# Splitting the operands of two 1x1 convolutions in a four-layer image kernel

## What is computed

```python
x = x + L0(gn(x))   # pooled mean -> gate g = sparsemax(8 experts); w_eff = g @ experts; 1x1 conv with w_eff
x = x + L1(gn(x))   # 3x3 depthwise conv, bias, bn, relu, prune (channel kept if its max >= 4.0);
                    # 1x1 conv pw_w, bias, bn, relu, prune (0.001)
x = x + L2(gn(x))   # q, k, v; squared and normalised q and k; kv = k2n^T v; attn = v + q2n kv; attn @ Wln + b
x = x + box3x3(gn(x))  # mean of the 3x3 neighbourhood
```

## Time and profile before

| | us |
|---|---|
| median of 3 runs | 1646.85 (1644.88 to 1647.62) |
| the profiled execution | 1646.53 |
| its span, first to last instruction | 1644.9 |
| PE busy | 1517.3 (92%) |
| DVE busy | 1296.9 (79%) |
| ACT busy | 1186.2 (72%) |
| POOL busy | 304.0 (18%) |

### The profile page before, as it was taken

The page is one execution under the profiler, slowest core; times in us unless marked ns, Lnnn a source line. Parts: engine busy times, 40 slices in busy tenths (PEclk is TensorE's granted clock), DMA queues, the critical chain, the costliest instruction groups (busy, mean ns, idle before and its releaser), DMA issues.

```text
span 1644.9 us, 27605 instructions
## 1 busy us (share of the span) xinstructions
PE 1517.3 (92%) x9282; PEld 1219.7 (74%) x9282; DVE 1296.9 (79%) x2339; ACT 1186.2 (72%) x2440; POOL 304.0 (18%) x238
## 2 busy tenths in 40 slices
PE   4469999999999999999999999999999999999850
PEld 2247787888887877878887877888877878878750
DVE  5758888888988888888888888889888888885430
ACT  3357777887777778877787778877787778776530
POOL 1100022222221121222221221222211221211001
PEclk8679999999999999999999999999999999999975
DMA  4001044434334444433334444333434444333435
GB/s 144 22 20 40 21 99 99 98 62 94 82 80 95 78 98 98 82 74 86 89 79 90 86 98 98 73 84 78 89 87 78 98 98 79 67 72 67 80 72 96
DMA packets 47172, 132.70 MB, mean 81 GB/s; under 512 B 3857, under 2 KB 4881, under 8 KB 47122
## 3 DMA queue, kind: packets, MB, share of 16 engines
q0 software_dynamic: 26112, 77.08, 28.8%
q1 hardware_dynamic: 20914, 54.98, 8.8%
q10 hardware_dynamic: 96, 0.00, 0.0%
HBM read 29.29 MB, written 102.76 MB: 80 GB/s over the span
## 4 chain that ended last, share of the span: by engine, by line
PE 90%; DVE 4%; DMA 2%; ACT 2%; issue 1%; POOLq 0%; ACTq 0%; DVEq 0%
PE conv_ps L457 35%; PE tile_ps L610 12%; PE tile_ps L539 10%; PE conv_ps L598 9%; PE small_ps L585 4%; PE tile_ps L484 4%; PE tile_ps L471 3%; PE tile_ps L567 3%; PE tile_ps L506 3%; DMA out<-row_sums 2%; PE tile_ps L503 2%; PE tile_ps L536 2%; PE tile_ps L555 2%; DVE h L803 1%; PE small_ps L448 1%
## 5 line engine op out<-in xcount | busy, mean ns | idle before, releaser
L803 DVE SCALAR_TENSOR_TENSOR h<-xpad,dw_sb,h 128x784 f32<-128x784 f32 x512 | 492.5, 1029 | 0.0
L1270 POOL DMA_DIRECT2D out<-row_sums x96 | 115.6, 1204 | 491.9 <-DMA out<-row_sums 411.2
L610 PE MATMUL tile_ps<-k,xT 112*128 112x256 f32 x896 | 201.4, 383 | 0.0
L1280 POOL TENSOR_SCALAR pw_masked<-pw_sb,hmask 128x256 f32<-128x256 f32 x64 | 118.4, 1857 | 385.4 <-DVE hmask L811 377.0
L610 PEld LDWEIGHTS tile_ps<-k,xT 112*128 112x128 f32 x896 | 171.9, 193 | 22.2
L539 PE MATMUL tile_ps<-wqk,xn_parts 128*112 128x256 f32 x1344 | 187.4, 294 | 0.0
L992 ACT ACTIVATE junk<-x 128x784 bf16<-128x784 f32 x192 | 162.8, 851 | 26.7 <-DVE x L830 17.5
L457 PE MATMUL conv_ps<-h,pw_masked 128*128 128x392 f32 x512 | 176.3, 498 | 5.5 <-issue 5.5
L598 PE MATMUL conv_ps<-x,mixed 128*128 128x392 f32 (+1 forms) x512 | 176.5, 498 | 2.2 <-ACT mixed L1029 1.1
L539 PEld LDWEIGHTS tile_ps<-wqk,xn_parts 128*112 128x112 f32 x1344 | 169.5, 175 | 0.1
L457 PE MATMUL conv_ps<-xn_parts,w_out 128*128 128x392 f32 x768 | 151.0, 345 | 0.0
(11 more groups left out here) (141 smaller groups left out, 2631.8 us busy)
## 6 DMA issues: line engine op xcount, KB each, us to landing
out<-row_sums POOLq DMA_DIRECT2D x96, 784.0 KB, 7.1
x<-x SPq DMA_DIRECT2D x32, 784.0 KB, 5.5
out<-x SPq DMA_DIRECT2D x32, 784.0 KB, 3.5
expert_sb<-expert_rows SPq DMA_DIRECT2D x8, 256.0 KB, 5.1
x<-w_qk SPq DMA_DIRECT2D x1, 512.0 KB
x<-w_vT SPq DMA_DIRECT2D x1, 256.0 KB
x<-w_ln SPq DMA_DIRECT2D x1, 256.0 KB
pw_sb<-pw_wT SPq DMA_DIRECT2D x1, 256.0 KB
```

What stands on the lines that cost most here:

```text
L610: mm = nc.tensor.matmul(tile_ps[:, KX_BANK, i * C:(i + 1) * C], xT[:, m, half(i)], k2[:, m, :], start=(m == 0), stop=(m == M - 1))
L803: ins = nc.vector.scalar_tensor_tensor(acc, view, scalar, acc, ALU.mult, ALU.add)
L1270: pool.dma_start(out_dram[F.times(1)], rows, accum_op=ALU.add).then_inc(rows_added[n].of(F), 16)
L1280: nc.gpsimd.tensor_scalar(pw_masked[:, j, :], pw_sb[:, j, :], hmask[:, j:j + 1], 0.0, ALU.mult, ALU.add).then_inc(pw_masked_ready.sem, 1)
```

## The change

Both plain float32 products become products on split operands.

- `pointwise` now multiplies `pw_parts` (the unmasked weights, split once in the set-up) by `h_parts`. The mask goes onto h: ScalarE's `h_high` writes h times hmask as high part, VectorE's `h_low` the low part. `mask_weights` on GpSimd goes. `h_parts` and `q_parts` are one buffer, `hq_parts`.
- `mixed_conv` multiplies `mixed_parts` (high by `scaled_mix` on ScalarE, low by `mixed_low` on VectorE) by `x0_parts`. The high part of x is written by the pass on ScalarE that sums x (`x0_high`, which stood among the key squares as half of `x0_sum` and now stands ahead of `sum_squares(1, A)`); the low part by `x0_low` on GpSimd, a `tensor_tensor` of 784 elements for each half, behind `add_rows`. The column of means that rides along with the product is split too (`mean_columns`, `mean_lows`). `x0_parts` has one buffer, so `x0_high` of an image waits for the first convolution of the image before, and `mixed_conv` waits for `mixed_low`, `mean_lows` and `x0_low`.
- x3 and the scratch tile `over` lose their second buffers. ScalarE's `sum_over_h` of the first half moves behind `normalise_x3`.
- The last two images (TAIL = 2) take `box_in_tail`: VectorE does the whole box filter in ten additions of 784 elements, and SyncE stores each half of the image once. These two images have no accumulating DMAs.

```diff
-x0 = sb("x0", [P, 2, J, XW])
-mixed = sb("mixed", [P, J * C])
+x0 = sb("x0", [P, 2, J, HW])
+x0_parts = sb("x0_parts", [P, 2, J, XW], F32R)
+mixed_parts = sb("mixed_parts", [P, 2, J * C], F32R)
...
-pw_masked = sb("pw_masked", [P, J, C])
...
-q_parts = sb("q_parts", [P, 2, J, HW], F32R)
-x3 = sb("x3", [P, 2, J, HW])
+hq_parts = sb("hq_parts", [P, 2, J, HW], F32R)
+h_parts, q_parts = hq_parts, hq_parts
+x3 = sb("x3", [P, J, HW])
...
+        if E.active and not E.in_tail:
             sp.wait_ge(x3_ready.sem, x3_ready.at(E))
...
+            sp.dma_start(out_dram[E.times(1)], x3[:]).then_inc(stored.of(E), 16)
+        if F.in_tail:
+            for j in range(J):
+                sp.wait_ge(tail_step.sem, tail_step.at(F - (IMAGES - TAIL), 5 * (j + 1)))
+                sp.dma_start(out_dram[F.offset][:, j, :], x3_of(F)[:, j, :]).then_inc(tail_stored, 16)
 
...
     def pointwise(C_, halves):
-        pe.wait_ge(h_ready.sem, h_ready.at(C_))
-        pe.wait_ge(pw_masked_ready.sem, pw_masked_ready.at(C_))
+        pe.wait_ge(h_lo.sem, h_lo.at(C_))
         for j in halves:
             wait_free((C_ - 1, q2_ready, j + 1), (C_ + 1, x1_ready, j + 1))
-            conv_tile(j, [(pw_masked[:, i, :], h[:, C_.odd, i, :]) for i in range(J)]).then_inc(pw_mm.sem, 1)
+            conv_tile(j, by_parts(pw_parts, h_parts)).then_inc(pw_mm.sem, 1)
...
-        pe.wait_ge(mean_column.sem, mean_column.at(A))
-        pe.wait_ge(mixed_ready.sem, mixed_ready.at(A))
+        pe.wait_ge(mean_low.sem, mean_low.at(A))
+        pe.wait_ge(x0_lo.sem, x0_lo.at(A))
+        pe.wait_ge(mixed_lo.sem, mixed_lo.at(A))
         for j in range(J):
             wait_free((A - 2, y_ready, j + 1), (A - 1, x1_ready, j + 1))
-            for i in range(J):
-                for a in range(2):
-                    more = a
-                    mm = nc.tensor.matmul(conv_ps[:, 2 * j + a, 0:HALF + more],
-                                          mixed[:, i * C + j * P:i * C + (j + 1) * P],
-                                          x0[:, A.odd, i, a * HALF:(a + 1) * HALF + more],
-                                          start=(i == 0), stop=(i == J - 1), skip_group_check=True)
+            for n, (u, v) in enumerate(((0, 0), (0, 1), (1, 0))):
+                for i in range(J):
+                    for a in range(2):
+                        width = HALF + 2 * a
+                        mm = nc.tensor.matmul(conv_ps[:, 2 * j + a, 0:width],
+                                              mixed_parts[:, u, i * C + j * P:i * C + (j + 1) * P],
+                                              x0_parts[:, v, i, a * HALF:a * HALF + width],
+                                              start=(n == 0 and i == 0), stop=(u == 1 and i == J - 1),
+                                              skip_group_check=True)
             mm.then_inc(conv0_mm.sem, 1)
...
+        parts_of(pw_parts, pw_raw)
         parts_of(wqk, wqk_raw)
...
         nc.vector.tensor_scalar(hmask[:], h_over[:], 0.0, None, ALU.is_gt).then_inc(hmask_step.sem, 1)
+
+    def h_low(C_):
+
+        for j in range(J):
+            dve.wait_ge(h_hi.sem, h_hi.at(C_, j + 1))
+            nc.vector.scalar_tensor_tensor(h_parts[:, 1, j, :], h[:, C_.odd, j, :], hmask[:, j:j + 1],
+                                           h_parts[:, 0, j, :].bitcast(F32), ALU.mult,
+                                           ALU.subtract).then_inc(h_lo.sem, 1)
...
+    def mean_lows(A):
+
+        dve.wait_ge(mean_column.sem, mean_column.at(A))
+        nc.vector.tensor_tensor(x0_parts[:, 1, :, HW:XW], gn_avg[:, 0, 0:2].unsqueeze(2).to_broadcast([P, J, 2]),
+                                x0_parts[:, 0, :, HW:XW].bitcast(F32), ALU.subtract).then_inc(mean_low.sem, 1)
+
+    def mixed_low(A):
+
+        dve.wait_ge(mixed_hi.sem, mixed_hi.at(A))
+        for i in range(J):
+            cols = slice(i * C, (i + 1) * C)
+            nc.vector.scalar_tensor_tensor(mixed_parts[:, 1, cols], small_ps[:, cols], gn_r[:, 0, i:i + 1],
+                                           mixed_parts[:, 0, cols].bitcast(F32), ALU.mult,
+                                           ALU.subtract).then_inc(mixed_lo.sem, 1)
...
     def make_x3(E):
-        if (E - 2).active:
-            dve.wait_ge(stored.of(E - 2), stored.at(E - 2))
-            dve.wait_ge(x3pad_ready.sem, x3pad_ready.at(E - 2))
-        for j in range(J):
+        if (E - 1).active and not (E - 1).in_tail:
+            dve.wait_ge(stored.of(E - 1), stored.at(E - 1))
+        for j in range(J):
+            if (E - 1).active:
+                dve.wait_ge(x3pad_ready.sem, x3pad_ready.at(E - 1, j + 1))
             dve.wait_ge(attn_mm.sem, attn_mm.at(E, j + 1))
-            nc.vector.scalar_tensor_tensor(split(x3[:, E.odd, j, :]), conv_banks(j), b_out[:, j:j + 1],
+            nc.vector.scalar_tensor_tensor(split(x3_of(E)[:, j, :]), conv_banks(j), b_out[:, j:j + 1],
                                            split(x2[:, E.odd, j, :]), ALU.add, ALU.add,
                                            accum_out=gn_in[:, 3, j:j + 1]).then_inc(x3_ready.sem, 1)
...
+    def box_in_tail(F):
+
+        s, turn = tail_step, F - (IMAGES - TAIL)
...
+        for j in range(J):
+            pad, rows, done = x3pad[:, j], row_sums[:, j], 5 * j
+            inner, out = pad[:, 1:1 + H, 1:1 + W], x3_of(F)[:, j, :]
+            dve.wait_ge(x3pad_ready.sem, x3pad_ready.at(F, j + 1))
+            nc.vector.tensor_tensor(rows[:, 1:1 + H, :], pad[:, 1:1 + H, 0:W], inner, ALU.add).then_inc(s.sem, 1)
+            dve.wait_ge(s.sem, s.at(turn, done + 1))
+            nc.vector.tensor_tensor(rows[:, 1:1 + H, :], rows[:, 1:1 + H, :], pad[:, 1:1 + H, 2:2 + W],
+                                    ALU.add).then_inc(s.sem, 1)
+            dve.wait_ge(s.sem, s.at(turn, done + 2))
+            nc.vector.tensor_tensor(inner, rows[:, 0:H, :], rows[:, 1:1 + H, :], ALU.add).then_inc(s.sem, 1)
+            dve.wait_ge(s.sem, s.at(turn, done + 3))
+            nc.vector.tensor_tensor(inner, inner, rows[:, 2:2 + H, :], ALU.add).then_inc(s.sem, 1)
+            dve.wait_ge(s.sem, s.at(turn, done + 4))
+            nc.vector.tensor_tensor(image_rows(out), image_rows(out), inner, ALU.add).then_inc(s.sem, 1)
...
             sparsemax(A)
+            mean_lows(A)
         if t.first:
             setup_weights()
...
         if C_.active:
             h_mask(C_)
-        if F.active:
+        if F.in_tail:
+            box_in_tail(F)
+        elif F.active:
             box_row_sums(F)
+        if C_.active:
+            h_low(C_)
+        if A.active:
+            mixed_low(A)
         if D.active:
             reciprocal_sums(D)
...
     def mean_columns(A):
 
         act.wait_ge(gn_read.sem, gn_read.at(A))
-        nc.scalar.copy(x0[:, A.odd, :, HW], gn_avg[:, 0, 0:2]).then_inc(mean_column.sem, 1)
+        if (A - 1).active:
+            act.wait_ge(conv0_mm.sem, conv0_mm.at(A - 1))
+        nc.scalar.copy(x0_parts[:, 0, :, HW:XW], gn_avg[:, 0, 0:2].unsqueeze(2).to_broadcast([P, J, 2])
+                       ).then_inc(mean_column.sem, 1)
...
+    def x0_high(Z):
+
+        act.wait_ge(x_loaded.of(Z), x_loaded.at(Z))
+        if (Z - 1).active:
+            act.wait_ge(conv0_mm.sem, conv0_mm.at(Z - 1))
+        for j in range(J):
+            nc.scalar.activation(x0_parts[:, 0, j, 0:HW], x0[:, Z.odd, j, :], ACT.Identity,
+                                 accum_out=gn_in[:, 0, j:j + 1]).then_inc(x0_hi.sem, 1)
+
+    def q_high(C_, D):
+        if C_.active:
+            act.wait_ge(pw_mm.sem, pw_mm.at(C_))
+        elif (D - 1).active:
             act.wait_ge(attn_mm.sem, attn_mm.at(D - 1))
         act.wait_ge(qa_ready.sem, qa_ready.at(D))
...
+    def h_high(C_):
+
+        act.wait_ge(hmask_step.sem, hmask_step.at(C_))
+        if (C_ - 2).active:
+            act.wait_ge(attn_mm.sem, attn_mm.at(C_ - 2))
+        for j in range(J):
+            nc.scalar.activation(h_parts[:, 0, j, :], h[:, C_.odd, j, :], ACT.Identity,
+                                 scale=hmask[:, j:j + 1]).then_inc(h_hi.sem, 1)
...
@@ -1182,23 +1288,23 @@
             relu_h(C_, 0)
         if D.active:
             x2_high(D)
-        if C_.active:
-            sum_over_h(C_, 0)
         if F.active:
             normalise_x3(F)
         if C_.active:
+            sum_over_h(C_, 0)
             relu_h(C_, 1)
         if A.active:
             scaled_mix(A)
         if C_.active:
             sum_over_h(C_, 1)
+            h_high(C_)
...
         for m in range(M):
             if D.active:
                 square_k(D, m)
-            if Z.active and 0 < m <= 2 * J:
-                x0_sum(Z, m - 1)
+            if Z.active and 0 < m <= J:
+                x0_squares(Z, m - 1)
...
         if t.first:
             act.wait_ge(setup_dve, SETUP_DVE)
+        if Z.active:
+            x0_high(Z)
         if A.active:
             junk_free((C_, gn_sums[2]), (Z, gn_sums[0]))
             sum_squares(1, A, x1[:, A.odd], x1_ready)
         if D.active:
```

(25 more changed lines are left out.)

90 lines of the change are left out of this document (46 added, 44 removed).

## The result

| | before | after |
|---|---|---|
| time, median of 4 runs each | 1647.23 us | 1672.13 us |
| ratio (95% interval) | | 1.0155 (1.0137 to 1.0172) |
| span of the profiled execution | 1644.9 us | 1671.3 us |

The runs answer the forecast of 1670 us closely. More than the total, the parts of it count. I cut both spans at the same operation, the copy of the group means that opens `variances` (line 713 before, 744 after), numbered by step. The profiled execution of the changed kernel took 1674.25 us, 2.1 over its median, so the parts add up to 26.5 us and not to the 24.9 of the medians.

What follows compares the result with a forecast made beforehand. Two bounds of equal length: TensorE's own work and a 46.40 us cycle through PE, ACT and DVE. 1646.5 + 32 (full steps) + 19 (start) - 27.7 (end) = 1670 us; range 1650 to 1699.

Steps and rivals of the forecast that it cites:

- The ring: Cycle from attention_out to the next: PE 16.58, ACT 9.42, DVE 20.40, together 46.40 us, within 0.05 of PE's own work.
- PE's 1.96 us: Time PE saves a step, 0.97 in pointwise and 0.99 in mixed_conv; only 0.1 us shortens the cycle, at relu_y.
- GpSimd's subtraction: x0_low blocks the six taps behind q_scales: first operation passes beside make_x1 and scale_q, taps lose 1.3 us a step.
- VectorE's 2.95 us hidden: h_low, mixed_low and mean_lows add 2.95 us between attention_weights_low and q_scales, covered by DVE's waits of 2.02 and 2.56.
- d: Duration of one x0_low operation on GpSimd: taken as 1.5 us, between 0.98 and 1.97; the skill's rate scaled gives 1.72.
- my formula: Loss of the six taps to the x0_low pair, 2d - 1.73: 1.3 us, between 0.25 and 2.2.
- The full steps: Steps t = 4 to 30, each about 1.2 us longer than 46.45: 27 x 1.2 = +32 us.
- The start: Steps 0 to 3: +9.3 as PE waits for mixed_low, +6.8, then +3; together +19 us, 14 to 23.
- The end: Last images with box_in_tail: ten additions of 1.0 us, half-image stores of 3.0; span ends 27.7 us earlier.
- One sign: PE idle about 3 us a step, most of it ahead of attention_out, with DVE's attn_parts as releaser.
- Rival 3: Both x0_low operations land among the taps (scale_q blocked or third DMA late): 3.0 us a step, 1720 us; chance 16%.

Runs made afterwards that it cites:

- experiment 1: Changed kernel, but GpSimd subtracts x's low part for the first image only (numbers wrong): 1631.24 us, ratio 0.991 to the kernel before.
- experiment 3: Two of the six taps behind q_scales moved ahead of it: changed kernel 1613.94 us (0.9797), kernel before 1644.12 us (0.9985).
- experiment 4: Changed kernel with the first of the first convolution's three products done twice, 8 more matmuls a step: 1674.34 us, ratio 1.0166.
- Experiment 5: Changed kernel, x's low-part subtraction moved: to VectorE ahead of nine taps, 1628.87 us; on GpSimd behind normalise_x1, 1774.72 us; on GpSimd beside nine taps, median 1744.56 us.
- experiment 6: Changed kernel, two taps moved ahead of q_scales, first mixed_low in setup_weights: GpSimd subtraction beside taps 1806.84 us, on VectorE 1618.31; kernel before, pointwise split, box_in_tail, moved taps: 1603.48.

## Why the prediction was right

**The ring.** It said that two rings of equal length bound a step and that PE's 1.96 us (measured: 1.80) are worth 0.1 us at most. Experiments 1, 3 and 4 show it: 46.35 us without GpSimd's subtraction, nothing from moved taps where PE is full, 1.9 us a step where it is not, and 1.5 us of extra matmuls for nothing.

**VectorE's 2.95 us hidden.** Right: with all of these operations in place experiment 1 has a period of 46.35, and the wait for `q_norm` is still 2.06 us. Experiment 5 spent that wait on 1.84 us more.

**GpSimd's subtraction.** The mechanism was right: the pair and the taps hold each other up, inside the ring. The size was right in part by luck. The term was d = 1.5 us an operation and a loss of 2d - 1.73 = 1.3; the taps lost 7.11 - 5.76 = 1.35. But an undisturbed pair takes 3.38 us, 1.7 an operation. POOL's timeline has one that runs while DVE waits 3.26 us ahead of the second `variances`:

```profile
47.53 3.38 POOL L1375 TENSOR_TENSOR x_parts<-x,x_parts 128x784 fp32r<-128x784 f32 x2 [34.68 <-ACT x_parts L1135]
```

With that pair my formula gives 1.65. It assumed that the pair runs through and the taps wait for its end, and that is not what happens. The two lines of the step shown above, with the shortest, median and longest duration in ns:

```profile
L834 DVE SCALAR_TENSOR_TENSOR h<-xpad,dw_sb,h x6: 1023/1023/2342, 825.9 to 832.0; 128x784 f32<-128x784 f32 x6
```

```profile
L1375 POOL TENSOR_TENSOR x_parts<-x,x_parts x2: 1851/2073/2295, 824.2 to 826.1; 128x784 fp32r<-128x784 f32 x2
```

The first tap (825.87) gets ahead of the second subtraction (826.07), which takes 2.30 us. One single tap, the second, then takes 2.34 us instead of 1.02, and that is the loss. An operation longer than I took, by 0.2 us, and an order that I did not foresee cancelled.

The first of the pair starts at 824.25, beside `scale_q`, which takes 1.84 us as in the earlier trace rows: it passes, as I took it to. By the Trainium skill (SBUF — State Buffer, "SBUF: two separate sides") the pair of ports shared by the two engines is an exclusive lock, held for a whole instruction; a VectorE operation takes it with two SBUF inputs or in a two-port mode, so `scale_q`, with one SBUF input, stays outside. The trace agrees, with 1.84 us beside GpSimd and 11.55 instead of 8.60 for taps. By the rate in the Trainium skill (GPSIMD Engine Reference, "Performance versus the Vector engine") d was an estimate of 1.72 and the total 12 us higher; the undisturbed pair's 1.69 is close to that rate, and the total did not follow because of the order just told.

**The full steps** came out 4.7 us over the forecast of 32. Two periods of 49.3 make 3.2 of that (last section); the rest is 1.24 a step in place of 1.2.

**The start** was right as a sum (18.4 for 19) and less so inside: the first step took 11.2 us for 9.3 and the second 4.1 for 6.8. In the first, PE started at 38.98 instead of 37.95 and took 7.30 us for the product instead of 6.56. In the second, I had let the `x0_low` of image 2 cost taps in full. In fact it stood behind them: the page gives line 1375 a longest duration of 7041 ns.

```profile
L1375 POOL TENSOR_TENSOR x_parts<-x,x_parts x64: 1565/1867/7041, 9.5 to 1447.9; 128x784 fp32r<-128x784 f32 x64
```

That row was the sign of the starvation that experiments 5 and 6 ran into.

**The end** was right to 1 us: ten additions of 0.98, stores of 2.3 instead of 3.0 us.

**One sign** came out otherwise: I had looked for most of PE's waiting ahead of `attention_out`, and it is 1.40 of 2.6 us there, the rest ahead of `attention_weights`.

**Rival 3** had the right mechanism for another placement: with both subtractions among taps, the taps lost 2.95 us, for which it had 3.0. What it lacked is that GpSimd can be the one that stands.

## What to carry to other kernels

An engine that is busy all the time is one bound; a cycle through other engines of the same length is a second, and time taken from the first is worth something only when the cycle gets shorter too, here by moving two taps into a wait of VectorE that already existed. A wait can be spent once: when the subtraction had used it, the same two taps gave nothing. And work sent to GpSimd because it is idle is not free where VectorE works on SBUF: here the taps and `q_low`, with two inputs there, lost time to it, and so did the first tap with one (1.93 instead of 0.61 us). Beside `scale_q`, with an input in PSUM, it cost nothing. The best kernel here left it out, which meant splitting one product and not the other.
